# Attention with a routed expert layer on one core: fresh blocks for the last two sequences, expert groups begun at the end of attention, and the shared expert placed among later groups

## The chip, the cores and the metric

The kernel runs on one core of one Trainium2 chip. The metric is device time in microseconds of one launch. A core has five engines with queues of their own: TensorE (PE), VectorE (DVE), ScalarE (ACT), GpSimd (POOL) and SyncE (SP), which here only issues DMAs.

## The reference

A transformer block over x of 16 sequences x 256 tokens x 128 channels. First attention with 16 heads of 64 on the layer-normed input, then, on the layer norm of the sum, 160 routed experts, 8 per token, and one shared expert.

```python
x = x + attn(layernorm(x), Wq, Wk, Wv, Wo, bo)         # softmax over 256 keys per sequence
h = layernorm(x)
probs = sigmoid(h @ router_w.T + expert_bias)          # 4096 tokens x 160 experts
top_w, top_idx = top_k(probs, 8)
top_w = top_w / (sum(top_w) + 1e-9) * 2.5
routed = sum over the 8 chosen e of top_w[e] * (silu(h @ w_gate[e].T) @ w_down[e].T)   # inner size 64
shared = silu(h @ w_gate_shared.T) @ w_down_shared.T
x = x + routed + shared
```

## The kernel before

**Attention.** The first stage walks through 16 sequences b of 8 steps g, a step being two heads. All engines run a software pipeline written out by hand (`body(b)`): sequences 0 to 3 are unrolled, 4 to 15 are a loop, and three more calls, `body(B)` to `body(B + 2)`, drain it. With a lag of one sequence come the second layer norm (DVE, with rs by POOL), its transpose (L456), router logits (L462) and the choice of 8 experts (DVE `best`, `choose`); with a lag of two come the ranks (PE, `ranks`), the slot numbers (DVE `distances`, `new_blocks`, `slot_numbers`, `best_slots`), the state (`new_state`), the table of blocks (`blocks`), and the weights (`weights`).

**Slots.** Each token is copied to 8 slots of slot_x in DRAM, by POOL's indirect DMAs (`scatter`, L829, 16 per sequence). Slots are grouped in blocks of 64, a block belongs to one expert; a partly filled block is filled up by later sequences. There are 672 blocks (512 for full ones and 160 for leftovers). slot_x and block_y are cleared with zeros during attention, since unused slots are read too.

**Shared expert.** After attention, x transposed for the whole batch lies in SBUF (xn2T_res, written by ACT at L680). Eight chunks of 512 tokens go through two products, a Silu and an addition to x_res (L1161).

**Groups.** The blocks are computed in 84 groups of 8. For group n, SP loads 256 KB of slot_x (L341), PE transposes it (L594), ACT evacuates (L709), DVE copies the 8 experts' weights from w_all in SBUF into a ring of four (`weights_of`, L1183), PE multiplies (`gates`, L604), ACT applies Silu, PE multiplies again (`downs`, L615), ACT evacuates (L724), SP stores 256 KB to block_y (L346). PE's order for slot n is transposes(n), gates(n-1), downs(n-2). DVE may copy for group n when downs(n-4) is done. Four groups are a turn.

**Gathers and combines.** POOL gathers, for each of the 32 token tiles, 8 rows per token from block_y (`gather`, L852, 8 indirect DMAs) into yg, a ring of four tiles. Before sequence b's first tile it waits until groups up to 4b + 23 are stored. A gather into a ring place waits for the combine of the tile four before. DVE's combine(k) weighs and adds the 8 rows (L1190 to L1200); it stands in DVE's queue after turn COMBINE_FROM + k (COMBINE_FROM = 9), and those left over come after the last turn.

**What sets the order.** Each engine's order is its program's. w_all comes in 16 DMAs of 10 experts, the last five (E_EARLY = 50) after attention, because w_all lies where attention's buffers were. SP loads the first group only when all 16 sequences are scattered and routed (L329 to L333). DVE begins the copies after the shared expert, the table blk_i (L1171), and `output_rows`, which turns slot numbers into rows of block_y.

## Time and profile before

| | us |
|---|---|
| median of 3 runs | 1104.2 (1103.73 to 1104.58) |
| the profiled execution | 1104.33 |
| its span, first to last instruction | 1102.4 |
| PE busy | 831.2 (75%) |
| DVE busy | 758.8 (69%) |
| POOL busy | 704.4 (64%) |
| ACT busy | 673.1 (61%) |
| TensorE's mean granted clock | 0.877 |

The profile is of one execution. A timeline row gives start, length, engine, line, operation, result and operands, count, and in brackets the idle time of the engine before it and what ended it ("issue": nothing that the profile shows). Times count from the span's start. PEclk or "granted clock" is TensorE's clock as a share of full speed (1.00 is 2.4 GHz, 0.50 is 1.2 GHz).

### The profile page before, as it was taken

The numbers are of one execution on the slowest core, as the hardware profiler recorded it, in microseconds if no ns is written. First come the engines' busy times: TensorE is split into PE (matmuls) and PEld (weight loads), VectorE is DVE, ScalarE is ACT, GpSimd is POOL, SyncE is SP. The second block draws the span as 40 slices with busy tenths as digits, with TensorE's granted clock in tenths as the row PEclk, the third lists the DMA queues.
The fourth block names the chain that finished last, engine by engine and source line by source line (L and its number), as shares of the span: only waits on it lengthen the run. The fifth ranks groups of instructions, "written<-read, shape, count | busy, mean of one in ns | idle before, by whom it ended". The sixth has DMA issues, their size and how long they took to land.

```text
span 1102.4 us, 28627 instructions
## 1 busy us (share of the span) xinstructions
PE 831.2 (75%) x8062; PEld 640.1 (58%) x8062; DVE 758.8 (69%) x2574; ACT 673.1 (61%) x1997; POOL 704.4 (64%) x892
## 2 busy tenths in 40 slices
PE   4999999999999999999999968899776770000000
PEld 4777777777777777777777744677565560000000
DVE  4568878778887887887877875577887884223223
ACT  5888888888888888888888851377664550000000
POOL 2235677676776667767667667103777777777775
PEclk9999999999999999999999995699998885555555
DMA  8814422323333311221212123388887762112111
GB/s 261 328 40 157 154 106 100 144 109 133 143 143 120 118 64 62 75 84 65 93 64 68 55 110 151 129 268 278 284 254 228 227 223 76 57 57 57 57 57 50
DMA packets 62457, 144.61 MB, mean 131 GB/s; under 512 B 12496, under 2 KB 18576, under 8 KB 62416
## 3 DMA queue, kind: packets, MB, share of 16 engines
q1 hardware_dynamic: 46032, 110.56, 28.5%
q0 software_dynamic: 16384, 33.59, 10.0%
q8 instruction: 16, 0.26, 0.1%
q14 instruction: 25, 0.20, 0.1%
HBM read 59.16 MB, written 84.93 MB: 131 GB/s over the span
## 4 chain that ended last, share of the span: by engine, by line
PE 57%; POOL 17%; issue 11%; DMA 6%; DVE 6%; ACT 2%; DVEq 1%; SPq 0%; POOLq 0%; ACTq 0%
POOL yg L852 14%; PE psS L406 11%; PE psO L483 10%; PE psT L431 8%; PE psY L397 8%; PE psVM L397 5%; PE psA L443 4%; DMA block_y<-y_b 4%; PE psS L604 2%; POOL slot_x L829 2%; PE psT L553 1%; PE psT L594 1%; DMA xb<-slot_x 1%; DVE w_b L1183 1%; ACT y_b L724 1%
## 5 line engine op out<-in xcount | busy, mean ns | idle before, releaser
L852 POOL DMA_INDIRECT yg<-block_y,tok_idx x256 | 252.1, 985 | 137.6 <-issue 79.0
L829 POOL DMA_INDIRECT slot_x<-xn_src,slot_u x240 | 244.0, 1017 | 99.2 <-issue 52.7
L675 ACT ACTIVATE p_sb<-psS,negmax 128x256 f32<-128x256 f32 x512 | 236.0, 473 | 95.8 <-DVE negmax L1118 93.8
L789 POOL TENSOR_SCALAR p_sb<-p_sb,rinv 128x256 f32<-128x256 f32 x256 | 138.9, 550 | 128.4 <-DVE rinv L1073 125.9
L1118 DVE TENSOR_REDUCE negmax<-psS 128x2 f32<-128x512 f32 x256 | 164.2, 682 | 37.5 <-PE psS L406 37.3
L1183 DVE COPY w_b<-w_all 128x192 f32 x672 | 135.1, 272 | 34.7 <-issue 30.5
L406 PE MATMUL psS<-qk_sb 64*128 64x256 f32 x1024 | 145.2, 402 | 2.6 <-ACT p_sb L675 2.6
L483 PE MATMUL psO<-pT_sb,v_sb 128*64 128x256 f32 x1024 | 138.8, 391 | 7.5 <-issue 5.5
L279 ACT COPY pT_sb<-psT 128x512 f32<-128x512 f32 x256 | 140.5, 615 | 1.4 <-PE psT L431 1.4
L431 PE MATMUL psT<-ident,p_sb 128*128 128x128 f32 x1024 | 132.7, 272 | 0.0
L1190 DVE TENSOR_TENSOR yg<-yg,wE_res 128x1024 f32<-128x1024 f32 x32 | 39.1, 1222 | 126.5 <-DMA yg<-block_y,tok_idx 126.0
L431 PEld LDWEIGHTS psT<-ident,p_sb 128*128 128x128 f32 x1024 | 114.8, 140 | 1.2 <-issue 0.8
L483 PEld LDWEIGHTS psO<-pT_sb,v_sb 128*64 128x64 f32 x1024 | 65.1, 136 | 67.0 <-issue 36.8
L675 ACT ACTIVATION_READ_ACCUMULATOR p_sb<-psS,negmax 128x1 f32 x512 | 104.0, 203 | 0.0
L406 PEld LDWEIGHTS psS<-qk_sb 64*128 64x128 f32 x1024 | 88.5, 186 | 25.3 <-issue 7.8
L604 PE MATMUL psS<-xbT,w_b 128*64 128x64 f32 x1344 | 62.8, 241 | 34.1 <-issue 25.6
L651 ACT COPY qk_sb<-psY 128x512 f32<-128x512 f32 x128 | 76.1, 595 | 7.3 <-PE psY L397 4.9
L604 PEld LDWEIGHTS psS<-xbT,w_b 128*64 128x64 f32 x1344 | 51.2, 149 | 50.6 <-issue 44.5
L443 PE MATMUL psA<-wo_sb,oT_sb 128*128 128x128 f32 x512 | 79.5, 278 | 0.5 <-DVE oT_sb L1124 0.5
L667 ACT ACTIVATE p_sb<-p_sb,rinv 128x256 f32<-128x256 f32 x128 | 71.0, 555 | 0.0
L443 PEld LDWEIGHTS psA<-wo_sb,oT_sb 128*128 128x128 f32 x512 | 67.2, 191 | 2.0 <-DVE oT_sb L1124 1.0
L1073 DVE RECIPROCAL rinv<-rowsum 128x4 f32<-128x4 f32 x128 | 22.7, 177 | 66.3 <-ACT p_sb L675 62.8
(159 smaller groups left out, 1720.3 us busy)
## 6 DMA issues: line engine op xcount, KB each, us to landing
block_y<-zero SPq DMA_DIRECT2D x21, 1024.0 KB, 4.0
xb<-slot_x SPq DMA_DIRECT2D x84, 256.0 KB
block_y<-y_b SPq DMA_DIRECT2D x84, 256.0 KB
w_all<-in_wgd_dram SPq DMA_DIRECT2D x16, 960.0 KB
slot_x<-zero SPq DMA_DIRECT2D x1, 11264.0 KB, 40.9
slot_x<-zero SPq DMA_DIRECT2D x10, 1024.0 KB
yg<-block_y,tok_idx POOLq DMA_INDIRECT x256
slot_x<-xn_src,slot_u POOLq DMA_INDIRECT x240
```

The lines of the kernel that those rows point to most:

```text
L279: copy(pT_sb[:, (g - 3) % 2, h].rearrange("p a t -> p (a t)"), psT[:, h, :]).then_inc(s[f"pt{h}_ok"], 1)
L397: m = pe.matmul(dst, wsl[a], xsl[c], start=(n == 0), stop=(n == 2))
L406: m = pe.matmul(psS[:, h, qt * SEQ:(qt + 1) * SEQ], qk_sb[r, par, 0, qt * P:(qt + 1) * P], qk_sb[r, par, 1, :], start=True, stop=True)
L431: m = pe.transpose(psT[:, h, kt * SEQ + qt * P:kt * SEQ + (qt + 1) * P], p_sb[:, (g - 3) % 2, h, qt, kt * P:(kt + 1) * P], ident[:])
L443: m = pe.matmul(psA[:, 0, i * P:(i + 1) * P], oT_sb[:, (g - 4) % 2, i * P:(i + 1) * P], wo_sb[:, gp, :], start=(gp == 0 and i == 0), stop= ...
L483: m = pe.matmul(psO[h * DH:(h + 1) * DH, 0, 0:SEQ], v_sb[:, (g - 3) // 2 % 2, kt, (g - 3) % 2, h * DH:(h + 1) * DH], pT_sb[:, (g - 3) % 2, ...
L675: act.activation(p_sb[:, (g - 1) % 2, h, qt, :], psS[:, h, qt * SEQ:(qt + 1) * SEQ], ACT.Exp, bias=negmax[:, (g - 1) % 2, h, qt:qt + 1], s ...
L789: pool.tensor_scalar(pq, pq, rinv[:, (g - 2) % 2, k // 2, k % 2:k % 2 + 1], 1.0, ALU.mult, ALU.mult).then_inc(s["pn_ok"], 1)
L829: pool.indirect_dma_start(slot_x, bass.IndirectOffsetOnAxis(ap=slot_u[:, int(last), i, j:j + 1], axis=0), (xn2 if last else xn2_src)[:, i, ...
L852: pool.indirect_dma_start(yg[:, r, k, :], None, block_y, bass.IndirectOffsetOnAxis(ap=tok_idx[:, par, r, k:k + 1], axis=0)).then_inc(gat[r ...
L1118: dve.tensor_reduce(negmax[:, (g - 1) % 2, h, :], psS[:, h, :].rearrange("p (i k) -> p i k", i=TB), AX.X, ALU.max, negate=True).then_inc(s ...
L1183: m = dve.tensor_copy(w_b[:, r, i, :], w_all[:, bass.ds(e, 1), :].rearrange("p o i -> p (o i)"))
```

## The change

- The last two sequences (14, 15) get blocks of their own. `seal()` resets the state ahead of sequence 14's numbers: no block has room and numbering begins at FRESH = 160 + 14 x 32 = 608. There are 832 blocks, so 104 groups and 26 turns.
- SP loads the first groups when the scatters of sequences 0 to 13 have landed. Only at turn 9 it waits for the others (a semaphore of their own, scat_l). 20 experts instead of 50 are loaded late, and those in the last step of attention.
- The drain is cut to four steps of `body(B)`. What was left of it, transposes, logits, choice, ranks, slot numbers and weights of sequence 15, is written between groups 0 and 13. The table is made in two parts, columns for blocks 0 to 511 first, the rest at group 13; `output_rows` comes after group 10. The gathers of sequences 14 and 15 wait for all stores.
- x transposed is not kept in SBUF: ACT issues a DMA to DRAM (ffn_xT) instead of the copy at L680. The shared expert is done in 16 chunks of 256 tokens, one per turn from turn 9 on: SP loads a chunk, PE's two products are in r = 2 and r = 3, ACT's Silu in r = 2, DVE's addition in the next turn after the copy of r = 0, and PE's transposes of that r = 0 wait for the addition before.
- COMBINE_FROM is 10. The ring of w_b runs backwards in memory. Buffers are placed in another order, and three are aliased. Fills are denser. POOL computes rs of the second norm ahead of the scatter at g = 3.

```diff
-NBLK = T * TOPK // HB + E
+NBLK = T * TOPK // HB + 2 * E
-E_EARLY = 50
+E_LATE = 20
+SEALED = B - 2
+FRESH = E + SEALED * SEQ_BLK
-COMBINE_FROM = 9
+COMBINE_FROM = 10
+LEAD, LATE_RANKS, LATE_TABLE = 4, 5, 13
...
@@ sync @@
-                sp.wait_ge(s["s_ps"], 3 * i + 28)
+                sp.wait_ge(s["s_ps"], 2 * i + 28)
...
-                sp.wait_ge(s["s_ps"], 4 * i + 68)
+                sp.wait_ge(s["s_ps"], 3 * i + 60)
...
-            with sp.Fori(0, (E - E_EARLY) // 10) as i:
-                sp.wait_ge(s["s_ps"], 8 * i + 160)
+            with sp.Fori(0, (E - E_LATE) // 10) as i:
+                sp.wait_ge(s["s_ps"], 8 * i + 140)
...
+            sp.wait_ge(s["yq_ps"], NSTEP)
+            sp.wait_ge(s["v_ps"], G // 2 * B)
+            sp.wait_ge(s["xt_lo"], B + 1)
+            for i in range(E_LATE // 10):
+                sp.dma_start(w_all[:, 10 * i:10 * i + 10], wgd[:, 10 * i:10 * i + 10]).then_inc(s["we_in"], 16)
+            sp.wait_ge(s["scat"], 16 * SEALED * TB * TOPK)
-            sp.wait_ge(s["wr_ok"], B)
-            sp.wait_ge(s["be_ok"], B)
-            sp.wait_ge(s["st_ok"], 3 * B)
-            sp.wait_ge(s["x2r_ok"], B)
-            sp.wait_ge(s["scat"], 16 * NT * TOPK)
...
+            def turn(it, chunk=None):
                 for r in range(RING):
                     load_group(it, r, False)
                     store_y(RING * it + (r - STORE_LAG), (r - STORE_LAG) % 2)
+                    if r == 1 and chunk is not None:
+                        wait(sp, s["sh_ps"], chunk)
+                        sp.dma_start(xs, xT[bass.ds(chunk, 1)].rearrange("o p t -> (o p) t")).then_inc(s["xs_in"], 16)
@@ tensor @@
+            def shared_hidden(n):
+                pe.wait_ge(s["xs_in"], 16 * (n + 1))
+                pe.matmul(psT[0:INTER, 1, 0:SEQ], wgs_sb[:], xs, start=True, stop=True).then_inc(s["sh_ps"], 1)
+            def shared_out(n):
+                for i in range(TB):
+                    m = pe.matmul(psT[:, 0, i * P:(i + 1) * P], hs[:, i * P:(i + 1) * P], wds_sb[:], start=True, stop=True)
                 m.then_inc(s["sho_ps"], 1)
...
+            def experts(it, chunk=None):
                 for r in range(RING):
                     n = RING * it + r
+                    early = n if isinstance(n, int) else None
+                    if r == 0 and chunk is not None:
+                        wait(pe, s["shared_ok"], chunk)
+                    if r == RING - 1 and chunk is not None:
+                        pe.wait_ge(s["hs_ok"], chunk + 1)
+                    if early == LATE_RANKS + 1:
+                        pe.wait_ge(s["d_ok"], B)
+                    if early == LATE_TABLE + 1:
+                        pe.wait_ge(s["tab_ok"], 2)
                     transposes(it, r, n)
+                    if early == 0:
+                        continue
+                    if early == 1:
+                        ffn_transposes(B)
+                        logits(B)
+                        pe.wait_ge(s["p_ok"], 4 * NSTEP)
+                    gates((r - 1) % RING, n - 1)
+                    if early == LATE_RANKS:
+                        pe.wait_ge(s["mask_ok"], B)
+                        ranks(psT[:, (r - 1) % 2, :])
+                    if early == LATE_TABLE:
+                        pe.wait_ge(s["be_ok"], B)
+                        table(psT[:, (r - 1) % 2, :], TABLE_A, BC)
+                    if r == RING - 2 and chunk is not None:
+                        shared_hidden(chunk)
+                    if r == RING - 1 and chunk is not None:
+                        shared_out(chunk)
...
+                    downs((r - 2) % RING, n - 2)
@@ scalar @@
+            def keep_input(b):
+                wait(act, s["x2t_ok"], b)
+                act.dma_start(ffn_xT.rearrange("(b p) t -> b p t", p=D)[bass.ds(b - 1, 1)].rearrange("o p t -> (o p) t"),
+                              xn2T[:]).then_inc(s["x2_st"], 16)
@@ gpsimd @@
-                    if not is_last(b, 1) or g != 3:
-                        scatter(b, g)
                     if g == 3 and seq(b, 1):
                         inverse_deviation(b - 1, "ln2", mv2, ve2, rs2)
-                    if is_last(b, 1) and g == 3:
-                        scatter(b, g)
+                    scatter(b, g)
...
+                    late = isinstance(b, int) and b >= SEALED
                     for k in range(2):
-                        wait_apart(pool, sty[k], 8 * SEQ_BLK // GB * b + 8 * (E + SEQ_BLK) // GB)
+                        wait_apart(pool, sty[k], 8 * NGRP if late else 8 * SEQ_BLK // GB * b + 8 * (E + SEQ_BLK) // GB)
@@ vector @@
+            def seal():
+                dve.wait_ge(s["st_ok"], 3 * SEALED)
+                dve.tensor_scalar(room[:], ones_row[:], -HALF_UP, None, ALU.mult).then_inc(s["seal_ok"], 1)
+                dve.tensor_scalar(n_taken[:], ones_row[:, 0:1], float(FRESH), None, ALU.mult).then_inc(s["seal_ok"], 1)
...
+            def turn(it, chunk=None):
                 for r in range(RING):
                     weights_of(r, RING * it + r, False)
+                    if r == 0 and chunk is not None:
+                        shared(chunk)
...
+            weights(B)
+            ffn_norm(B)
+            dve.wait_ge(s["b_ps"], 1)
+            table(psY[:, 0, :], 0, TABLE_A)
+            dve.wait_ge(s["tab_ok"], 1)
+            dve.wait_ge(s["we_in"], 16 * (E // 10))
+            group(0)
+            biased(B)
+            group(1)
+            best(B)
+            blocks(B)
+            group(2)
+            choose(B)
+            group(3)
...
+            group(5)
+            distances(B + 1, psT[:, (LATE_RANKS - 1) % 2, :])
+            new_blocks(B + 1)
+            group(6)
+            slot_numbers(B + 1)
+            best_slots(B + 1)
+            group(7)
+            chosen(B + 1)
+            best_places(B + 1)
+            group(8)
+            blocks(B + 1)
+            group(9)
+            weights(B + 1)
+            group(10)
+            output_rows()
...
+            group(13)
+            dve.wait_ge(s["b_ps"], 2)
+            table(psT[:, (LATE_TABLE - 1) % 2, :], TABLE_A, BC)
```

## Rows read from the trace of the kernel before

**Rows 1.** Page, slices: POOL's busy tenths and the granted clock in 40 slices of 27.6 us.
```profile
POOL 2235677676776667767667667103777777777775
PEclk9999999999999999999999995699998885555555
```

**Rows 2.** Page, the chain that ended last, by line (share of the span).
```profile
POOL yg L852 14%; PE psS L406 11%; PE psO L483 10%; PE psT L431 8%; PE psY L397 8%; PE psVM L397 5%; PE psA L443 4%; DMA block_y<-y_b 4%; PE psS L604 2%; POOL slot_x L829 2%; PE psT L553 1%; PE psT L594 1%; DMA xb<-slot_x 1%; DVE w_b L1183 1%; ACT y_b L724 1%
```

**Rows 3.** Waits: who waited for whom, us in total, times, longest.
```profile
POOL yg L852 <- DMA block_y<-y_b: 58.1, 5, 54.8
PE psVM L456 <- DVE xn L894: 10.7, 13, 6.1
```

**Rows 4.** Timeline of POOL: last scatter; gathers of tiles 0, 4, 16, 20, and the last.
```profile
694.23 0.95 POOL L829 DMA_INDIRECT slot_x<-xn,slot_u  x1 [0.30 <-issue]
...
758.19 1.03 POOL L852 DMA_INDIRECT yg<-block_y,tok_idx  x1 [54.75 <-DMA block_y<-y_b]
...
799.70 1.03 POOL L852 DMA_INDIRECT yg<-block_y,tok_idx  x1 [0.27 <-POOL tok_idx L841]
...
931.17 1.89 POOL L852 DMA_INDIRECT yg<-block_y,tok_idx  x1 [1.64 <-issue]
...
973.33 0.97 POOL L852 DMA_INDIRECT yg<-block_y,tok_idx  x1 [1.35 <-issue]
...
1094.44 0.94 POOL L852 DMA_INDIRECT yg<-block_y,tok_idx  x1 [0.30 <-issue]
```

**Rows 5.** Timelines of POOL, DVE and PE around L456 in one sequence of attention.
```profile
580.10 1.05 POOL L829 DMA_INDIRECT slot_x<-xn_src,slot_u  x1 [0.17 <-DVE mv L887]
582.35 0.60 DVE L894 TENSOR_SCALAR xn<-x_res,mv,rs 128x128 f32 x2 [0.79 <-POOL rs L762]
583.01 0.44 PE L456 MATMUL psVM<-ident,xn 128*128 128x128 f32 x2 [0.29 <-DVE xn L894]
```

**Rows 6.** Timeline of DVE from the end of attention to the first groups.
```profile
654.34 0.25 DVE L887 BATCH_NORM_AGGREGATE mv<-st 128x2 f32<-128x6 f32 x2
658.71 0.60 DVE L894 TENSOR_SCALAR xn<-x_res,mv,rs 128x128 f32<-128x128 f32 x2 [4.13 <-POOL rs L762]
...
662.12 0.49 DVE L1102 TENSOR_TENSOR z_sb<-psVM,eb_sb 128x320 f32<-128x320 f32 x1
...
675.52 0.18 DVE L1058 TENSOR_TENSOR wE_res<-w_e,winv 128x16 f32<-128x16 f32 x1
...
701.06 0.29 DVE L1145 TENSOR_SCALAR yg<-pos_u 128x256 uint32<-128x256 uint32 x1
...
702.66 0.43 DVE L1156 TENSOR_TENSOR pos_u<-yg 128x256 uint32<-128x256 uint32 x1
```

**Rows 7.** Timeline of DVE, weight copies of groups 8, 23 and 28.
```profile
718.45 1.44 DVE L1183 COPY w_b<-w_all 128x192 f32 x8 [0.68 <-PE psA L615]
...
747.20 1.44 DVE L1183 COPY w_b<-w_all 128x192 f32 x8 [0.33 <-issue]
...
756.89 1.44 DVE L1183 COPY w_b<-w_all 128x192 f32 x8 [0.66 <-issue]
```

**Rows 8.** Timeline of DVE: a shared addition; the starts of combines 0, 3 and 11.
```profile
688.02 0.69 DVE L1161 TENSOR_TENSOR x_res<-psT,x_res 128x512 f32 x1 [3.21 <-PE psT L553]
...
780.91 1.22 DVE L1190 TENSOR_TENSOR yg<-yg,wE_res 128x1024 f32<-128x1024 f32 x1
...
812.74 1.21 DVE L1190 TENSOR_TENSOR yg<-yg,wE_res 128x1024 f32<-128x1024 f32 x1
...
906.60 1.23 DVE L1190 TENSOR_TENSOR yg<-yg,wE_res 128x1024 f32<-128x1024 f32 x1
```

**Rows 9.** Gates at either clock; window: PE, PEld, DVE, ACT, POOL busy, clock, DMA.
```profile
707.35 1.12 PE L604 MATMUL psS<-xbT,w_b 128*64 128x64 f32 x16
867.03 0.69 PE L604 MATMUL psS<-xbT,w_b 128*64 128x64 f32 x16 [3.00 <-issue]
781.00:910.00 129.00, 95.79 (x1657) 73.06 (x1652) 108.55 (x412) 71.46 (x187) 97.94 (x99) 0.88 0.75 238
```

More of the change, by code:

```diff
@@ L507, in values_read, with ffn_transposes, logits, ranks @@
                 wait(pe, s["v_ok"], min(G // 2 * b + n, G // 2 * B) if isinstance(b, int) else G // 2 * b + n)
[L509 removed]
+            def ffn_transposes(b):
+                wait(pe, s["ln2_xn"], TB * b)
                 for i in range(TB):
[L512 removed]
+                    m = pe.transpose(psVM[:, 0, i * P:(i + 1) * P], xn2[:, i, :], ident[:])
+                m.then_inc(s["x2t_ps"], 1)
+            def logits(b):
+                wait(pe, s["x2t_ok"], b)
+                for i in range(TB):
+                    m = pe.matmul(psVM[:, 0, i * E:(i + 1) * E], xn2T[:, i * P:(i + 1) * P], rw_sb[:],
+                                  start=True, stop=True)
+                m.then_inc(s["lg_ps"], 1)
+            def ranks(ps):
+                for i in range(TB):
+                    o = ps[:, i * E:(i + 1) * E]
                     m = pe.matmul(o, tri[:], mask[:, i, :], start=True, stop=(i == 0))
@@ L519, in ranks, with table @@
                 m.then_inc(s["rk_ps"], 1)
+            def table(ps, c0, c1):
+                for c in range(c0, c1):
+                    n = min(P, NBLK - c * P)
+                    m = pe.matmul(ps[:, (c - c0) * P:(c - c0) * P + n], blk_e[:, c:c + 1].broadcast_to([P, P]), ident[:, 0:n],
+                                  start=True, stop=True)
+                m.then_inc(s["b_ps"], 1)
             def input_transpose(b):
@@ new lines, in experts @@
+                    if early == 3:
+                        pe.wait_ge(s["ot_ok"], NSTEP)
+                        pe.wait_ge(s["x1_ok"], B)
+                    downs((r - 2) % RING, n - 2)
+            pe.wait_ge(s["pt0_ok"], NSTEP)
+            pe.wait_ge(s["pt1_ok"], NSTEP)
+            for it in range(LEAD):
+                experts(it)
+            with pe.Fori(LEAD, COMBINE_FROM - 1) as it:
+                experts(it)
+            experts(COMBINE_FROM - 1, 0)
+            with pe.Fori(COMBINE_FROM, TURNS - 1) as it:
+                experts(it, it - (COMBINE_FROM - 1))
@@ L921, in _, with biased @@
             dve.wait_ge(s["b_dve"], 1)
+            def biased(b):
+                wait(dve, s["lg_ps"], b)
+                wait(dve, s["den_ok"], b - 1)
+                dve.tensor_tensor(z_sb[:], psVM[:, 0, 0:TB * E].rearrange("p (i e) -> p i e", i=TB), eb_sb[:],
+                                  ALU.add).then_inc(s["z_ok"], 1)
             def best(b):
@@ L1018, in blocks @@
                 n = b - 1
-                first = bass.ds((b - 2) // 4, WIN)
+                late = isinstance(b, int) and b - 2 >= SEALED
+                first = bass.ds(WIN_LATE if late else (b - 2) // 4, WIN)
                 dve.tensor_copy(blk_w[:], blk_num[:, first]).then_inc(s["bw_ok"], 1)
@@ L1136, in body @@
                         choose(b)
-            sequences(dve, body)
+            for b in range(4):
+                body(b)
+            with dve.Fori(4, B) as b:
+                body(b)
+            body(B, 4)
             def output_rows():
```

310 lines of the change are left out of this document (145 added, 165 removed).

## Prediction

> **What bounds the kernel now.** I read the slices of the page first: PE at full clock up to slice 23, a gap of two slices at half clock, then the expert groups up to about 910 us, and from there only POOL busy (seven tenths and more) with PE idle [rows 1]. The chain of work that ended last says the same: POOL's gathers (L852) are its largest line [rows 2]. POOL waited once, 54.8 us, for the store of block_y, and then never for long again [rows 3]. The POOL timeline gives the skeleton [rows 4]: the last scatter begins at 694.23, the first gather at 758.19, the 256th and last at 1094.44. So the time is (start of the first gather) + (256 gathers) + (a rest of 1102.4 - 1095.4 = 7.0). 32 tiles of 8 gathers take 337 us: tiles 0 to 15, beside the groups, 931.17 - 758.19 = 173.0, or 10.8 each; tiles 16 to 31 take 164.2, or 10.26 each. Whatever moves the first gather moves the end, as long as nothing holds POOL later. Two things can: a gather of tile k+4 waits for combine k (four yg buffers), and the last tiles wait for the last groups' stores.
>
> The profiled execution took 1104.33 for a span of 1102.4, so 1.9 lie around it; the median is 1104.2. I sum in the span and add 1.9.
>
> **Part 1: attention.** PE is full there, so only a PE wait is worth anything. In each sequence DVE waits 0.79 us for POOL's rs before it writes xn2 (582.35), and PE then waits for xn2 (583.01); POOL starts a scatter at 580.10 ahead of ve and rs [rows 5]. The change puts inverse_deviation ahead of that scatter at g = 3. PE's wait at L456 is 10.7 us in 13 times, 6.1 of it the last [rows 3], so 4.6/12 = 0.38 per sequence. Moving rs by one scatter (1.3 us) covers it. I take 4 us off the end of attention (bounds: 0, if another wait takes its place, and 6). POOL's later scatters go 1.3 us later and have slack. ACT loses a copy per sequence (L680) and issues a DMA instead; ACT never issues a DMA in this trace, SP's issues take about as long as that copy did, so I take zero, bounds -0.4 to +0.4 per sequence on ACT, which has slack at g = 5. The zero fills grow (52 instead of 42 MB, and denser), but they go by DMA beside a PE that is full anyway: nothing. Aliases (moved, le, z_sb in place) only repeat orders that DVE's queue has already.
>
> **Part 2: the start of the groups.** Before, DVE copies the first weights after 703.09, the end of the slot arithmetic [rows 6]. In between lie the second layer norm (xn2 at 658.71), the last sequence's routing (662.12 to 675.7), and the shared expert. Now the groups start behind xn2. Work on DVE from there to the copy of group 23, in its written order:
> - xn2 done at 658.71 + 0.60 = 659.3, minus 4 of part 1: 655.3. The weights of the sequence before (1.3) fit into the 4.13 that DVE waits for POOL there [rows 6].
> - the first table, 0.7.
> - 24 groups: from 718.45 to 756.89 there are 20 in 38.4 us, 1.92 each [rows 7], so 46.1; the first one costs 1.5 more (registers, cold code).
> - routing of the last sequence: 13.6 less new_state (0.7), plus blocks(B) 1.6, output_rows 2.0, late table 0.3 [rows 6]: 16.8.
> - hand-overs where DVE has to wait until PE comes to ranks (group 5), the late table (group 13) and where PE waits in turn: bounds 0 and 10, taken as 4, two group times.
> Sum: 655.3 + 0.7 + 46.1 + 1.5 + 16.8 + 4 = 724.4. Before, group 23 was copied at 747.20 + 1.44 = 748.6 and the first gather came at 758.19, 9.5 later [rows 4, 7]; now PE is less behind, I take 8.6. **First gather at 733**, 25 us earlier; bounds 727 and 745. Table and weights are no limit: the last loads of w_all are issued in the last attention step. Nor is POOL: its scatter for the last sequence waits for slot numbers after group 6, about 680, and 16 scatters take 20 us.
>
> **Part 3: the coupled stretch.** DVE does four groups, then one combine. Combines start at 780.91 and, eleven rounds later, at 906.60: 11.43 us a round, and the last eight from 812.74 average 11.73 [rows 8]. POOL needs only 10.8 a tile, so DVE is slower than POOL, but before this lasted 12 rounds with a head start: combine 0 began 22.7 after the first gather, while tile 4 started 41.5 after it. The change takes from both sides. There are 20 more groups, so 16 rounds (26 turns less 10). COMBINE_FROM is 10: four more groups before combine 0, at (780.91 - 758.19)/11 = 2.07 each, 8.3, so combine 0 starts 31 + 0.3 after the first gather. And each round gains the shared chunk: half of an L1161 addition (0.69 for 512 columns [rows 8]), so 0.4, and 0.1 around it.
>
> A wait is new: at r = 0 PE's transposes wait for that addition, which stands on DVE behind the copy of group r = 0. Queued behind it on PE are gates and downs of the two groups before, which formerly ran under the combine; DVE's copies of r = 2 and 3 wait for those downs. Now PE stands idle 3.0 us for the first copy after the combine [rows 9]; it would be idle some 5 and start a slot later. With slots of 1.9 and copies of 2.0 the ring still just keeps up, so bounds of the cost per round are 0 and 2 and I take 0.1 to 0.2. **Round: 11.7 + 0.5 + 0.1 = 12.3.**
>
> Combine 15 is then through at 31.3 + 15 x 12.3 + 2.9 = 218.7 after the first gather. Unheld, POOL would start tile 19 at 173.0 + 3 x 10.5 + 1 = 205.5 [rows 4]. It is held back 13 us. From there 13 tiles at 10.26, 133.4, and the rest of 7.0.
>
> The last sequences' blocks cost nothing themselves: all 104 groups are stored some 230 after the first gather, tile 28 comes at 312. The fresh blocks mean only that many more groups. The removed shared stage (661 to 697) is in part 2 already.
>
> **Sum.** 733 + 218.7 + 133.4 + 7.0 = 1092.1 in the span, **1094.0** in time: 25 gained at the start, 15 given back in the rounds. The rounds decide: 15 x 1 us. Break-even is at a round of 12.3 + 10.3/15 = 13.0.
>
> **A rule weighed.** POOL's gathers beside copies: one row is 0.94 to 0.97 when alone, tiles beside the groups cost 0.5 more [rows 4]. The Trainium skill, "SBUF — State Buffer", section "SBUF: two separate sides", says that a DVE instruction such as an fp32 copy within SBUF locks GpSimd out of the port pair it needs for writing DMA descriptors, and the other way round, for the whole instruction. By that rule more groups beside gathers are a price of this change: tiles 16 to 19 at 10.8 instead of 10.26, 2 us. Since POOL is held anyway in those tiles, the sum stays; without holding it would be 2 us more, which the second rival contains.
>
> **Rivals.**
> (a) *PE's clock makes it the bound (slower).* Between 781 and 910 the granted clock was 0.88 on average, after PE had been busy 96 of 129 us; in the slices ahead of them, with steady groups, it was nine tenths or more [rows 1, 9]. At the lower of the two levels (1.2 GHz) 16 matmuls of L604 take 1.12 instead of 0.69 [rows 9], 1.6 times, so a slot 3.1 instead of 1.92. With the new wait PE has four slots after the addition and idles longer in one piece, so the clock should fall in more rounds. Then copy r = 3 waits for PE and the next addition for shared_out: 4 x 3.1 + 1.5 + 0.7 = 14.6 a round. If two rounds in three go so, the mean is 13.8: 1094 + 15 x 1.5 = **1116**. It decides from 13.0 on, a third of the rounds. Against it: a slow PE is a busy PE, and in the trace the clock came back each time. The Trainium skill, "TensorE: Matmul & The Clock Gate", section "HAM oscillation — how this bites in real kernels", describes this: bursts with waits between them are throttled anew in every iteration. Chance 0.17.
> (b) *Gathers alone are the bound.* If rounds stay under 11.7 (POOL held means fewer stretched copies), nothing holds POOL: 733 + 173.0 + 164.2 + 2 + 7.0 + 1.9 = **1081**. For it: copies take 1.44 per 8 before the gathers begin [rows 7]. Chance 0.17.
> (c) *The early start is eaten.* Hand-overs, cold straight-line code and half clock put the first gather at 745, the upper bound: **1106**. The 3.5 us that POOL once lost at new code, in the 4.13 of [rows 6], show such a price. Chance 0.14.
> (d) *The change doesn't hold the groups' early start at all* (DVE waits for the last w_all load): the sum is (c) or worse; 0.02, with (c).
> Forecast as it stands: 0.5, its own range 1086 to 1102.
>
> **How the numbers follow.** Range 1081 to 1108: from (b) to the beginning of (a). 0.2% (2.2 us, about what a measurement of this kernel can tell from no change) puts "same" at 1102.0 to 1106.4. Faster: forecast 0.49 + (b) 0.17 + a little of (a) and (c) 0.03 = 0.69. Same: 0.11, most of (c). Slower: 0.20, (a) and the end of (c).
>
> **What the profile will show.** First gather at 727 to 739 (part 2). PE without idle at L456 and attention's end 4 us earlier (part 1). Combines 31 us after the first gather and then every 12.3 (part 3), with POOL waiting for them from tile 8 or so, 13 us in all; the granted clock there 0.8 to 0.9. Wrong would be: a first gather after 745, rounds over 13 with a clock of 0.7, or POOL idle at its last tiles for stores.

## The result and the profile after

| | before | changed |
|---|---|---|
| median | 1104.04 (1103.73 to 1104.58) | 1122.48 (1118.91 to 1123.47) |
| ratio, 95% interval | | 1.0161 [1.0138, 1.0183] |
| span of the profiled execution | 1102.4 | 1120.5 |
| PE / DVE / POOL busy | 831.2 / 758.8 / 704.4 | 868.7 / 794.1 / 704.9 |
| granted clock | 0.877 | 0.893 |

The change makes the kernel slower by 1.6%. The forecast was 1094.0, and the time lies above the range's end of 1108. POOL's timeline shows the skeleton that the sum was built on, as in [rows 4]: first gather, tile 20, last gather.

```profile
720.40 1.01 POOL L909 DMA_INDIRECT yg<-block_y,tok_idx  x1 [25.71 <-DMA block_y<-y_b]
...
991.01 0.97 POOL L909 DMA_INDIRECT yg<-block_y,tok_idx  x1 [1.34 <-issue]
...
1112.53 0.95 POOL L909 DMA_INDIRECT yg<-block_y,tok_idx  x1 [0.30 <-issue]
```

The first gather is 37.8 us earlier than before, more than forecast. Tiles 4, 8, 12, 16 and 19 begin at 761.92, 814.06, 874.71, 936.19 and 977.53. Tiles 4 to 19 take 215.6 us for 15 tiles, 14.4 each, where before a tile took 10.8. So all that was gained at the start, and more, is lost again there. The page's slices, as in [rows 1], show both: the two slices at five and six tenths of the clock are now one at six tenths, and POOL is at five tenths in the middle of the gathers.

```profile
POOL 2236676767767676776767755277555454577775
PEclk9999999999999999999999968998887887855555
```

The chain that ended last, by line, as in [rows 2]:

```profile
PE psS L419 12%; PE psO L494 11%; PE psT L444 9%; PE psY L410 9%; POOL yg L909 9%; DVE w_b L1253 6%; PE psVM L410 5%; PE psA L456 5%; DVEq L249 3%; PE psS L603 3%; PE psT L593 3%; PE psY L614 2%; DVE yg L1260 2%; DVEq L1253 1%; DVE yg L1262 1%
```

POOL's gathers fell from 14% to 9% of it, and DVE's weight copies rose from 1% to 6%: through the coupled stretch the path now runs over DVE and the groups. The waits (who waits for whom: us in total, times, longest), as in [rows 3]:

```profile
POOL yg L909 <- issue: 93.7, 238, 9.7
PE psT L593 <- DVE x_res L1242: 69.2, 16, 9.1
DVE w_b L1253 <- issue: 49.4, 74, 5.6
POOL yg L909 <- DMA block_y<-y_b: 43.7, 7, 25.7
```

The second is the change's new wait: PE's transposes (L593) stand for 69.2 us in 16 times, 4.3 each, until DVE's addition (L1242) is done. Combines start at 755.53, 769.36, 782.86, 796.36, 810.11, 824.13, 837.86, 851.86, then 870.75, 885.42, 899.02, 913.09, then 932.23, 946.67, 960.30, 974.03. Two rounds, into combines 8 and 12, take 18.89 and 19.14 us; the other thirteen take 13.5 to 14.7, 13.88 on average. Forecast was 12.3 for all.

DVE's and PE's timelines over one ordinary round (the last instruction of a combine begins at 758.28; L1253 are the weight copies r = 0 to 3, L603 gates, L593 transposes, L578 shared_out, the second of the shared expert's two products):

```profile
756.04 0.71 PE L578 MATMUL psT<-wds_sb,x_res 64*128 64x128 f32 x4
759.03 1.67 DVE L1253 COPY w_b<-w_all 128x192 f32 x8 [0.45 <-issue]
760.62 0.41 DVE L1242 TENSOR_TENSOR x_res<-psT,x_res 128x256 f32<-128x256 f32 x1
761.26 1.11 PE L593 MATMUL psT<-ident,xb 128*128 128x128 f32 x4 [3.92 <-DVE x_res L1242]
761.33 1.45 DVE L1253 COPY w_b<-w_all 128x192 f32 x8 [0.29 <-issue]
762.30 1.12 PE L603 MATMUL psS<-xbT,w_b 128*64 128x64 f32 x16
764.41 1.11 PE L593 MATMUL psT<-ident,xb 128*128 128x128 f32 x4
765.29 1.66 DVE L1253 COPY w_b<-w_all 128x192 f32 x8 [2.51 <-PE psVM L614]
765.46 0.69 PE L603 MATMUL psS<-xbT,w_b 128*64 128x64 f32 x16
```

PE has nothing to do once the downs behind shared_out are through, although the gates of one group and the downs of the one before it are ready to run: they stand behind the transposes. After the addition PE runs its first slot at half clock (L603 takes 1.12, not 0.69; in all 15 rounds the first gates behind this wait take 1.09 to 1.12), a slot lasts 3.1 us, and DVE's copy r = 2 waits 2.51 us for the downs (L614) in it. This wait of DVE comes to 34.0 us in 17 times, the longest 2.6.

### The profile page after: what moved, and what is told of

It is laid out like the page before. It is cut to its first block, busy times and chain, and to the rows that moved or that the text cites. A ratio compares the mean times of both kernels' runs of the same rounds, so it can differ in the third digit from the quotient of the medians.

```text
span 1120.5 us, 30801 instructions
## 1 busy us (share of the span) xinstructions
PE 868.7 (78%) x8800; PEld 673.4 (60%) x8800; DVE 794.1 (71%) x2741; ACT 703.0 (63%) x2069; POOL 704.9 (63%) x892
## 4 chain that ended last, share of the span: by engine, by line
PE 61%; DVE 12%; POOL 10%; issue 10%; DVEq 5%; ACT 1%; DMA 0%; POOLq 0%; ACTq 0%
PE psS L419 12%; PE psO L494 11%; PE psT L444 9%; PE psY L410 9%; POOL yg L909 9%; DVE w_b L1253 6%; PE psVM L410 5%; PE psA L456 5%; DVEq L249 3%; PE psS L603 3%; PE psT L593 3%; PE psY L614 2%; DVE yg L1260 2%; DVEq L1253 1%; DVE yg L1262 1%
## 5 line engine op out<-in xcount | busy, mean ns | idle before, releaser
L1253 DVE COPY w_b<-w_all 128x192 f32 x832 | 171.0, 277 | 88.8 <-issue 49.4
L1195 DVE TENSOR_REDUCE negmax<-psS 128x2 f32<-128x512 f32 x256 | 164.3, 683 | 28.6 <-PE psS L419 28.4
L593 PE MATMUL psT<-ident,xb 128*128 128x128 f32 x416 | 80.2, 324 | 71.2 <-DVE x_res L1242 69.2
L751 ACT COPY xbT<-psT 128x512 f32<-128x512 f32 x104 | 61.5, 592 | 81.5 <-PE psT L593 81.2
L593 PEld LDWEIGHTS psT<-ident,xb 128*128 128x128 f32 x416 | 51.5, 160 | 93.5 <-issue 83.3
L603 PE MATMUL psS<-xbT,w_b 128*64 128x64 f32 x1664 | 82.5, 250 | 15.5 <-issue 8.1
L603 PEld LDWEIGHTS psS<-xbT,w_b 128*64 128x64 f32 x1664 | 67.8, 158 | 38.7 <-issue 32.8
L456 PE MATMUL psA<-wo_sb,oT_sb 128*128 128x128 f32 x512 | 78.8, 276 | 0.5 <-DVE oT_sb L1201 0.5
```

What stands on the lines that cost most here:

```text
L593: m = pe.transpose(psT[:, par, i * P:(i + 1) * P], xb[:, r, i, :], ident[:])
L603: m = pe.matmul(psS[half, par, cols], w_b[:, RING - 1 - r, i, 0:INTER], xbT[:, par, :, i * P // GB:(i + 1) * P // GB], start=True, stop=True)
L1195: dve.tensor_reduce(negmax[:, (g - 1) % 2, h, :], psS[:, h, :].rearrange("p (i k) -> p i k", i=TB), AX.X, ALU.max, negate=True).then_inc(s ...
L1253: m = dve.tensor_copy(w_b[:, RING - 1 - r, i, :], w_all[:, bass.ds(e, 1), :].rearrange("p o i -> p (o i)"))
```

## Experiments

Ratios are to the kernel before on the same chip, which took 1103.7 (numbers 1, 3, 4, 5), 1104.1 (2, 6, 7, 8) and 1103.6 (9, 10). "Ordinary" rounds are those other than into combines 8 and 12. The changed kernel itself was measured once, beside the kernel before at 1104.04; where an experiment is compared with it, the two come from different chips. PE has a last wait for the additions ahead of the last turn; it is written apart and stays in experiments 4, 8, 9 and 10, so the round into combine 15 still has it there (13.70, 14.13, 14.66 and 14.41 us).

**1. POOL's order in attention alone.** In the kernel before:

```diff
-                    if not is_last(b, 1) or g != 3:
-                        scatter(b, g)
                     if g == 3 and seq(b, 1):
                         inverse_deviation(b - 1, "ln2", mv2, ve2, rs2)
-                    if is_last(b, 1) and g == 3:
-                        scatter(b, g)
+                    scatter(b, g)
```

> The kernel before with one edit: POOL computes rs of the second norm ahead of the scatter at g = 3. In the changed kernel a sequence of attention takes 39.0 us instead of 39.65, 10 us in all. Theory A: the order on POOL brings all of it: 39.0 per sequence and about 1094.5 in time, since the later stages only shift. Theory B: ACT's copy that became a DMA brings the part over my 0.38 per sequence: 39.3 here and about 1098.5.

1098.15, ratio 0.9939 [0.9916, 0.9962]. A sequence takes 39.30 instead of 39.65, the last layer norm's aggregate comes at 648.62 instead of 654.34 [rows 6], the first gather at 752.80. So this edit gives the 0.35 a sequence that the forecast had worked out (0.38), and no more: the changed kernel's 39.0 has a second cause.

**2. ACT's copy replaced as well.** Experiment 1, and in it the copy of L680 becomes a DMA that ACT issues (whoever waits for it counts to 16 a sequence, and ACT waits for it before it writes xn2T again):

```diff
-                        act.copy(xn2T_res[:, bass.ds((b - 1) * SEQ, SEQ)], xn2T[:]).then_inc(s["x2r_ok"], 1)
+                        act.dma_start(xn2T_res[:, bass.ds((b - 1) * SEQ, SEQ)], xn2T[:]).then_inc(s["x2r_ok"], 16)
```

> As the run of this kernel before, at the usual speed: the kernel before with rs first and ACT's copy as a DMA. Theory A (the copy is the rest of attention's gain): 39.0 per sequence, 1093.5. Theory B: 39.3, 1098.

1090.33, ratio 0.9884 [0.9856, 0.9912]; a sequence takes 39.05, the aggregate comes at 646.53, the first gather at 746.91. ACT's copy is the second cause, 0.25 a sequence. What it cost were PE's small gaps: between 194 and 620 us PE is busy 421.00 of 426 us in experiment 1 and 424.07 here (the columns are PE, PEld, DVE, ACT, POOL busy, clock, DMA share, GB/s).

```profile
194.00:620.00 426.00, 421.00 (x3347) 330.94 (x3346) 348.41 (x1152) 363.51 (x1118) 300.96 (x412) 1.00 0.28 99
```

```profile
194.00:620.00 426.00, 424.07 (x3372) 333.87 (x3370) 351.09 (x1165) 362.93 (x1118) 303.66 (x415) 1.00 0.29 103
```

Of the 5.9 us by which the first gather comes earlier than in experiment 1, 2.1 lie ahead of the aggregate. The other 3.8 fall between it and the gather; their cause is not shown.

**3. No chunks among the groups.** In the changed kernel the 16 chunks, their waits and loads are taken out of the turns, so the shared expert is missing from the output:

```diff
-                    if r == 0 and chunk is not None:
-                        wait(pe, s["shared_ok"], chunk)
...
-                        shared_hidden(chunk)
...
-                        shared_out(chunk)
...
-                    if r == 0 and chunk is not None:
-                        shared(chunk)
```

> The changed kernel without the shared expert among the groups (its sum is left out: no chunk loads, no products, no Silu, no additions, no wait of PE). Theory A (PE's wait for the addition makes the rounds long): rounds fall from 13.9 to 11.5 to 11.8 and the time by 15 x 2 = 30 us or more, to 1085 or less. Theory B (16 rounds beside 20 more groups are slow by themselves, by clock or DMA): rounds stay at 13 or more, time over 1105. Theory C, on the two rounds of 19: if the longer loop body of DVE makes them, they go with the additions (the body is then as in the kernel before), another 10 us less; if they come from the loop's start over alone, they stay.

1082.36, ratio 0.9806 [0.9787, 0.9825]. Ordinary rounds take 11.48, the two long ones 14.72. The rounds are long because of the chunks; the two longer ones exist without them, though shorter than with them (18.89 and 19.14).

**4. No wait of PE.** DVE's addition reads x_res alone, so the shared sum is missing from the output; the products, the Silu and an instruction of DVE in the addition's place stay:

```diff
-                    if r == 0 and chunk is not None:
-                        wait(pe, s["shared_ok"], chunk)
...
-                dve.tensor_tensor(xr, psT[:, 0, 0:SEQ].rearrange("p (i d) -> p i d", i=TB), xr, ALU.add).then_inc(s["shared_ok"], 1)
+                dve.tensor_tensor(xr, xr, xr, ALU.max).then_inc(s["shared_ok"], 1)
```

> The changed kernel, all of its shared work kept, but DVE's addition reads x_res alone instead of PSUM (the shared sum is left out of the output), so PE's transposes need not wait for it. Theory A (the wait is the cost): rounds 12.0 to 12.4 apart from the two long ones, time about 1122 - 13 x 1.6 = 1101, and the granted clock between the combines higher. Theory B (the additions, products and the Silu themselves are the cost, or the clock falls anyway under the combines): rounds over 13, time over 1113. The two rounds of 19 stay in any case.

1090.97, ratio 0.988 [0.9851, 0.9909]. Ordinary rounds 11.83, long ones 16.44 and 16.58; combine 0 to combine 15 takes 186.9 us instead of 218.5. Of the 39.8 that experiment 3 takes off this stretch, 31.6 are the wait, and 8.2 the chunks' own work, 0.55 a round. The time is lower than either theory had it, and so are the rounds. The window from combine 0 to combine 15 speaks on the clock; the changed kernel first, then this one:

```profile
755.53:974.03 218.50, 150.14 (x2258) 111.48 (x2260) 147.36 (x571) 99.53 (x256) 121.94 (x128) 0.83 0.63 194
```

```profile
756.36:943.23 186.87, 143.98 (x2258) 106.30 (x2259) 147.61 (x572) 98.09 (x255) 125.06 (x129) 0.86 0.74 228
```

The mean clock rises from 0.83 to 0.86. The mean alone does not tell how long a round is: over the same stretch it is 0.85 in experiment 3, with ordinary rounds of 11.48, and 0.94 in experiment 9, with 12.95.

**5. The addition ahead of the copy.** DVE's order alone, nothing left out:

```diff
                 for r in range(RING):
-                    weights_of(r, RING * it + r, False)
                     if r == 0 and chunk is not None:
                         shared(chunk)
+                    weights_of(r, RING * it + r, False)
```

> The changed kernel with DVE's addition ahead of the copy for r = 0 instead of behind it, nothing left out. Theory A: PE's wait ends a copy and its register loads earlier, 2 to 3 us; the round falls from 13.9 to 12.4 to 12.9 and the time by 15 to 22 us, to 1100 to 1108. Theory B (the wait is not what counts): no change, 1120 or more; or worse, if DVE then waits for shared_out.

1088.46, ratio 0.9871 [0.984, 0.9902]. Ordinary rounds 11.63, long ones 15.25 and 15.45. One instruction moved ahead of a copy of 1.7 us takes 34 us off the changed kernel and makes it faster than before, by more than the 15 to 22 us that theory A had. PE still waits for the addition, 42.4 us in all instead of 69.2, but DVE's waits for downs (L614, whichever PSUM tile they write) come to 4.5 us instead of 38.1, and the clock between combines 0 and 15 is 0.90.

**6. DVE's loop written out.** In the changed kernel:

```diff
-            with dve.Fori(1, (TURNS - COMBINE_FROM) // YR) as q:
+            for q in range(1, (TURNS - COMBINE_FROM) // YR):
```

> As the run of this kernel before, on a chip where the kernel before should take its usual 1104: DVE's loop over the coupled rounds written out. Theory A (the loop's start over costs 5.3 and 5.6): both long rounds fall to 13.9, time 1112. Theory B: they stay, 1122. In the run where everything was slow the rounds at combines 8 and 12 were no longer than the others, 19.4 and 19.6, which speaks for A.

1109.54, ratio 1.0055 [1.0036, 1.0074]. The rounds into combines 8 and 12 take 13.85 and 14.04, like the others (13.62). DVE's timeline shows what is gone. The first copies after combines 7 and 11 in the changed kernel:

```profile
860.28 1.67 DVE L1253 COPY w_b<-w_all 128x192 f32 x8 [5.26 <-issue]
...
921.89 1.55 DVE L1253 COPY w_b<-w_all 128x192 f32 x8 [5.64 <-issue]
```

and those after combines 7 and 11 with the loop written out:

```profile
859.77 1.69 DVE L1253 COPY w_b<-w_all 128x192 f32 x8 [0.46 <-issue]
...
913.98 1.57 DVE L1253 COPY w_b<-w_all 128x192 f32 x8 [0.58 <-issue]
```

**7. Both, 5 and 6.**

> As the run of this kernel before, at the usual speed: addition ahead of the copy of r = 0 and DVE's loop written out. Theory A: 6 to 7 less than with the addition ahead alone (1088.5), so 1082. Theory B, straight-line code costs as much as the loop's start over: 1088.

**1072.85, ratio 0.9713 [0.9682, 0.9745]**: 2.9% faster than before and 4.4% faster than the changed kernel. All 15 rounds average 11.16. The two edits give 51.2 us of the 218.5 between combines 0 and 15; singly they gave 36.6 and 13.5. The time is some 9 us below the 1082 of theory A. The start of tile 20:

```profile
942.03 0.97 POOL L909 DMA_INDIRECT yg<-block_y,tok_idx  x1 [1.34 <-issue]
```

Tile 20 begins 220.3 after the first gather (721.73), where the changed kernel's begins 270.6 after; from the start of the first gather to that of the last it is 341.0 us, where before it was 336.3 [rows 4]. POOL is hardly held. This is the second rival's case (gathers alone are the bound), reached with another order.

**8. PE's wait half filled.** 16 transposes of the identity, into a part of psT that nobody reads then, ahead of the wait in each turn of the loop:

```diff
+                    if r == 0 and chunk is not None and not isinstance(it, int):
+                        pe.wait_ge(s["xt2_ok"], n)
+                        for _ in range(16):
+                            pe.transpose(psT[:, 1, 0:P], ident[:], ident[:])
                     if r == 0 and chunk is not None:
                         wait(pe, s["shared_ok"], chunk)
```

> As the run of this kernel before, at the usual speed: 16 transposes ahead of PE's wait. Theory A (clock): L603 behind the wait takes 0.69 instead of 1.1, rounds fall by 1.0 to 1.5 and the time to 1100 to 1108. Theory B (latency of the handover): rounds stay at 13.9 or grow, 1122 or more.

1118.18, ratio 1.0123 [1.009, 1.0155]; ordinary rounds 13.55, clock 0.89 over the stretch. In the ordinary rounds 1.6 to 3.3 us of the wait were left, and in about half of them the clock still fell, at once or one slot later. Neither theory's number, so this run decides nothing.

**9. PE's wait filled.** The same with `range(32)`.

> The kernel of g1_busy_32 again, on another chip, for the same reason: 32 transposes of the identity ahead of PE's new wait in each coupled turn, which fill it; order unchanged. Theory Q: ordinary rounds 13.4 to 14.0 and 1114 to 1126, although the gates behind the wait take 0.69 us. Theory C: ordinary rounds 12.8 or less, 1106 or less.

1111.09, ratio 1.0059 [1.0042, 1.0077]. PE's and DVE's timelines over one round (L626 are the transposes put in; lines of DVE carry L1257 and L1246 here):

```profile
785.80 3.71 PE L626 MATMUL psT<-ident 128*128 128x128 f32 x32
787.45 1.91 DVE L1257 COPY w_b<-w_all 128x192 f32 x8 [0.47 <-issue]
789.28 0.41 DVE L1246 TENSOR_TENSOR x_res<-psT,x_res 128x256 f32<-128x256 f32 x1
789.92 0.65 PE L593 MATMUL psT<-ident,xb 128*128 128x128 f32 x4 [0.40 <-DVE x_res L1246]
790.50 0.69 PE L603 MATMUL psS<-xbT,w_b 128*64 128x64 f32 x16
792.59 1.76 DVE L1257 COPY w_b<-w_all 128x192 f32 x8 [1.46 <-PE psVM L614]
```

In the ordinary rounds, the last one apart, PE waits 1.8 us at most, the first gates behind the wait take 0.69 in all but one, and the clock over the stretch is 0.94. DVE's copy r = 2 still waits for the downs, 1.46 us here instead of 2.51. Ordinary rounds take 12.95, or 12.8 without the last, whose wait is not filled. That is between the theories: the order alone forecast 13.4 to 14.0, the clock alone 12.8 or less, and the time, too, is between 1106 and 1114. Holding the clock is worth 0.93 a round, or 1.1 without the last.

**10. The wait moved behind gates and downs.** PE's order in r = 0 of a turn with a chunk, DVE's as in the changed kernel:

```diff
                     if r == 0 and chunk is not None:
+                        gates((r - 1) % RING, n - 1)
+                        downs((r - 2) % RING, n - 2)
                         wait(pe, s["shared_ok"], chunk)
+                        transposes(it, r, n)
+                        continue
```

> The kernel of g2_wait_later again, on another chip: there the kernel before itself took 1258.68 and every kernel's rounds were near 20 us, so that nothing about the wait could be read. The edit: PE's new wait kept, but in the turns with a chunk the gates of r = 3 and the downs of r = 2 of the turn before are issued ahead of it, the transposes of r = 0 behind it; nothing left out. Theory Q (order: the downs behind the wait are what costs): ordinary rounds 11.9 to 12.5, time 1088 to 1098. Theory C (clock after the idle time): ordinary rounds 13.2 or more, time 1110 or more.

1097.98, ratio 0.9956 [0.994, 0.9973]; ordinary rounds 12.27, as the theory of the order forecast. One round:

```profile
783.79 1.67 DVE L1257 COPY w_b<-w_all 128x192 f32 x8 [0.45 <-issue]
785.38 0.41 DVE L1246 TENSOR_TENSOR x_res<-psT,x_res 128x256 f32<-128x256 f32 x1
785.73 3.48 DVE L1257 COPY w_b<-w_all 128x192 f32 x16
786.03 1.06 PE L593 MATMUL psT<-ident,xb 128*128 128x128 f32 x8 [2.87 <-DVE x_res L1246]
```

PE still waits, 2.87 us. The clock between combines 0 and 15 is 0.87, a little over the changed kernel's 0.83 and well under experiment 9's 0.94. But the copies r = 1 and r = 2 now run in one piece behind the addition: what copy r = 2 needs was done under the combine.

**11. The same edits where the kernel before is slow.** In two further sets of runs the kernel before itself took 1256.5 us (the first four below) and 1258.7 us (the last three). The record numbers their chips 10 and 2, and it gives the number 2 to experiments 9 and 10 as well, where the kernel before took 1103.6 some minutes later. So it is not shown that the chip makes the difference, although the expectations of 9 and 10 speak of another chip. The edits are those above: the loop written out (6), with the addition first (7), the wait half filled (8), ACT's DMA (2), the wait filled (9), the wait moved (10), and 7 and 10 together.

> The changed kernel with DVE's loop over the coupled rounds 4 to 15 written out, nothing left out. DVE stood 5.3 and 5.6 us idle where that loop starts over (combines 8 and 12), and 3.3 longer than usual still without the additions. Theory A (going back to the loop's start costs it, as code is fetched anew): both go, combine to combine 13.9 throughout, time 10 us less, 1112. Theory B (something else comes in every fourth round, such as the slot copy of POOL or a DMA): they stay, 1122.

1.0245 [1.0203, 1.0287].

> The changed kernel with DVE's addition ahead of the copy of r = 0 and DVE's loop written out. In the run with the addition ahead alone the long rounds were 15.3 and 15.5 against 12.0. If both effects are separate: 3.3 x 2 = 6.6 less than that run, 1082 in time; if the fetch of straight-line code costs as much as the loop's start over, 1088 as there.

1.022 [1.0178, 1.0262].

> The changed kernel with 16 transposes of the identity into a PSUM bank that is free at that time, which PE does just ahead of its wait for DVE's addition, in the coupled turns: PE is then idle for a shorter piece. Theory A (the long wait costs through the clock: at 1.2 GHz the first slots behind it take 2.7 instead of 1.9, and DVE's copy of r = 2 waits 2.2 for them): the clock stays up, L603 behind the wait takes 0.69, rounds fall by 1.0 to 1.5, time 1100 to 1108. Theory B (the handover's latency costs it at any clock): rounds stay at 13.9, or grow by what the transposes delay, time 1122 or more.

1.0335 [1.0291, 1.0378].

> The kernel before with rs first (as in the first run) and ACT's copy of xn2T in each sequence replaced by a DMA that ACT issues, within SBUF. Theory A (the rest of attention's gain, 0.3 per sequence, is ACT's copy): 39.0 per sequence instead of 39.3, end of attention 4.5 us earlier, time 1093.5. Theory B (something else of the change brings it): 39.3, 1098.

0.9966 [0.9948, 0.9984].

> The changed kernel with 32 transposes of the identity (they write to a part of psT that nobody reads then) ahead of PE's new wait in each coupled turn, twice as many as in f3_busy_wait; 16 of them took 1.97 us there at half clock, and 2.09 us of waiting were left, so 32 fill the wait of 3.7 to 3.9 us nearly. Theory Q (queue: the wait costs because the gates and downs of the two groups before stand behind it, and DVE's copy r = 2 needs those downs; the clock hardly matters): ordinary rounds stay at 13.4 to 14.0 and the time at 1114 to 1126. Theory C (clock: the wait costs because PE stands idle in one piece and then runs its first slots at the lower level): slots behind the wait have gates of 0.69 us, ordinary rounds come down to 12.8 or less, the time to 1106 or less.

1.0401 [1.0379, 1.0423]. (The expectation calls 1.97 us for 16 transposes half clock; four of L593 take 0.65 in the same rounds and 1.11 at the lower level, so 1.97 is full clock.)

> The changed kernel with PE's new wait kept, but in the turns with a chunk the gates of r = 3 and the downs of r = 2 of the turn before are issued ahead of it, and the transposes of r = 0 behind it; DVE's order is that of the changed kernel, nothing is left out. Theory Q: the downs that copy r = 2 needs are done under the combine, its wait (2 to 2.5 us) is gone; ordinary rounds 11.9 to 12.5 as without the wait (11.9), time 1088 to 1098. Theory C: PE still stands idle for about 2.5 us or more in one piece and restarts at the lower level; ordinary rounds stay at 13.2 or more, time 1110 or more.

1.026 [1.0223, 1.0297].

> f2_both (addition ahead of copy r = 0, DVE's loop written out) and PE's wait moved behind gates and downs as in g2_wait_later; nothing left out. In f2_both POOL was nearly never held, so both theories expect about the same time: 1066 to 1073, rounds 10.8 to 11.2. Over 1076 would mean that the transposes of r = 0 have become late for ACT and for the gates one slot on.

1.0279 [1.0235, 1.0324].

The rounds of the last three and of the first take 17 to 22 us. PE's gates are broken up there by idle time in which it waits for nothing that the profile shows. With the loop written out, gates come in pieces:

```profile
966.07 0.85 PE L603 MATMUL psS<-xbT,w_b 128*64 128x64 f32 x16
968.96 0.80 PE L603 MATMUL psS<-xbT,w_b 128*64 128x64 f32 x9
970.48 0.34 PE L603 MATMUL psS<-xbT,w_b 128*64 128x64 f32 x4 [0.72 <-issue]
971.90 0.34 PE L603 MATMUL psS<-xbT,w_b 128*64 128x64 f32 x3 [1.07 <-issue]
```

What makes these gaps was not tried, so these ratios say little about the causes above. They do say that the gain of experiment 7 does not hold everywhere: under these conditions its kernel is 2.2% slower than before.

## Why the prediction was wrong

In the sum's own terms, of the profiled execution:

| term | forecast | measured | difference |
|---|---|---|---|
| first gather | 733 | 720.4 | -12.6 |
| from there to combine 0 | 31.3 | 35.1 | +3.8 |
| 15 rounds | 184.5 | 218.5 | +34.0 |
| combine 15 to tile 19 | 2.9 | 3.5 | +0.6 |
| 13 tiles | 133.4 | 136.0 | +2.6 |
| rest | 7.0 | 7.0 | 0 |
| span | 1092.1 | 1120.5 | +28.4 |

The skeleton held: POOL is held by combine 15, and from there on the tiles run alone. Two steps failed, both in the 15 rounds: 13 x (13.88 - 12.3) = 20.5 for the new wait, 2 x (19.0 - 12.3) = 13.4 in the two long rounds, of which some 3 are the same wait and 10 something that the sum did not contain. That the first gather came 12.6 early was not forecast either; without it the miss would have been larger by as much.

**The price of PE's wait (part 3).** The forecast named the right thing, gates and downs of two groups behind the wait and copies r = 2 and 3 behind those downs, had bounds of 0 and 2 for it, and took 0.1 to 0.2. Measured by experiment 4, it is 31.6 us in 15 rounds, 2.1 each, just over the upper bound. (The round without it was forecast at 11.7 + 0.5 = 12.2 and ordinarily took 11.83; that hid a part of the error.) The step that failed is "with slots of 1.9 and copies of 2.0 the ring still just keeps up". The ring has no slack there: what ran under the combine (3.0 us) and copy r = 0 (1.7) are two slots that the wait moves out of it, and they then come one after the other with copies that need them. Two runs split the 31.6. With the wait left and the order changed (10), 27.4 are gone; with the order left and the clock held (9), 13.2 are gone. Together that is 9 more than the whole, since they overlap: a slot at half clock costs DVE something only while DVE waits for it. So the order carries 18.4 to 27.4 of the 31.6, and the lower clock after the wait 4.2 to 13.2, the upper end being the 0.9 a round of experiment 9. That a slot at half clock counts only there is argued from the rows, not tried by itself.

**The start over of DVE's loop (nowhere in the sum).** DVE stands idle for 5.26 and 5.64 us where its loop over q starts over. Written out (6), both are gone. The kernel before had such a loop too. It started over once, after combine 7, and there DVE's gap was small, so no row of before showed this price (its other first copies after a combine wait 0.5 to 1.3):

```profile
865.21 1.73 DVE L1183 COPY w_b<-w_all 128x192 f32 x8 [1.56 <-issue]
```

In the changed kernel without chunks (3), whose loop holds the same kinds of instructions as the one before, the gaps are 4.32 and 4.27. So the additions in the body are at most a part of it; why the loop before was cheap stays open. The Trainium skill, "Runtime: NRT & Kernel Launch", section "Instruction fetch mechanics", says that instructions are fetched ahead in sequence and that a taken branch whose target is not in the current window makes the engine wait for a fetch. By that rule a body of four turns and four combines pays at each start over, if it is longer than the window, and straight code does not; the changed kernel agrees, the loop of before shows that it need not be so.

**The rivals.** (a) gave 1116 from a mean round of 13.8 and is closest in number, but its mechanism holds by half only: PE is busy 150.14 of the 218.5 us between combines 0 and 15 and is not the bound, DVE's wait is for downs behind the wait (r = 2, not r = 3 as the rival had it), and the clock there was 0.83, where the forecast had named 0.7 as the sign of this rival. Experiment 9 gives its share, 0.93 a round of the 1.58 that the ordinary rounds were over the forecast, and part of that share goes with the order as well. The rule of the Trainium skill cited there ("TensorE: Matmul & The Clock Gate", section "HAM oscillation — how this bites in real kernels"), that bursts with waits between them are throttled anew in each iteration, agrees with the round above (1.12 behind a wait of 3.92) and with what filling the wait takes away (0.69). (b) was right on what lies below: with both edits the time is 1072.85, where its 1081, less the 11.3 by which that run's first gather (721.73) came before 733, is 1069.7. (c) went the other way, and (d) did not come about: the first copy of weights begins at 648.36.

**Part 2, the first gather.** It came 12.6 before the forecast, outside its bounds (727 to 745). The last layer norm's aggregate came at 644.03, 10.3 earlier than before and not 4:

```profile
646.00 0.60 DVE L951 TENSOR_SCALAR xn<-x_res,mv,rs 128x128 f32<-128x128 f32 x2 [0.50 <-POOL rs L818]
...
648.36 1.65 DVE L1253 COPY w_b<-w_all 128x192 f32 x8 [1.16 <-issue]
...
710.78 1.44 DVE L1253 COPY w_b<-w_all 128x192 f32 x8 [0.54 <-issue]
```

That is 6.3 more than the forecast had. From the aggregate to the end of xn2 it is 2.57 us instead of 4.97, since DVE waits 0.50 for POOL where it had waited 4.13 [rows 6]: 2.4 more. From the end of xn2 (646.6) to the end of group 23's copy (712.2) there are 65.6 us instead of 69.1, and the gather follows 8.2 later instead of 8.6: -3.9. 6.3 + 2.4 + 3.9 = 12.6.

**Part 1, attention.** The size of POOL's order was right (experiment 1: 0.35 a sequence, forecast 0.38). The step that failed is ACT's: for a DMA issue in place of a copy the forecast took zero between bounds of -0.4 and +0.4, and experiment 2 gives 0.25 to the good. "PE is full there, so only a PE wait is worth anything" was too strict: no wait of PE for ACT stood among the long ones, yet PE's idle time between 194 and 620 us fell by 3.1 us with that copy gone.

**Part 3, the rest.** The chunk's own work was right: 0.55 a round (forecast 0.5). Combine 0 came 3.8 later after the first gather, since from group 23's copy to it there are 20 groups in 44.75 us, 2.24 each, instead of 2.07. The 13 tiles took 2.6 more: tile 19 itself takes 13.5.

**The rule weighed.** The prediction weighed the Trainium skill's rule on the port that DVE and GpSimd share ("SBUF — State Buffer", section "SBUF: two separate sides"). Copies take 1.44 before the first gather (710.78) and mostly 1.6 to 1.7 beside gathers, so they are longer by a sixth, which agrees in kind. Of the gathers no run shows a price: the changed kernel's tiles 0 to 2, beside copies, take 10.09, 10.05 and 10.12 us, and most tiles take 10.0 to 10.3 alone. With both edits tiles 12 to 14, where POOL is not held, take 10.47, 10.26 and 10.52, so the 2 us that the prediction set for four tiles is an upper bound. It decided nothing.

## What to carry to other kernels

Ask of a new wait not only how long it is but what stands behind it in its engine's queue, and who needs that; then put in front of it whatever does not need it (10), or let the instruction that it waits for run first (5). When the path runs through an engine's loop of long straight bodies, look for a gap at its start over, and write the loop out where it shows. A price between bounds of 0 and 2 us that is paid in every round is the forecast itself: here the range had to reach to 15 x 2 on the slow side.

## What the runs showed of the hardware

- A start over of DVE's loop took 5.26 and 5.64 us, and 4.32 and 4.27 in the kernel without chunks; the kernel before had 1.56 at the start over of a loop of the same kind.
- After 3.92 us without work TensorE ran its next slot at the lower of its two levels (16 gates in 1.12 us instead of 0.69), although over the whole stretch it had work for 69% of the time. With 3.71 us of transposes in such a wait it ran at full clock behind it (0.69).
- A DMA issued by ACT in place of a copy within SBUF made a sequence of attention 0.25 us shorter, on a PE without a long wait.
- The same kernel before took 1256.5 and 1258.7 us in two sets of runs and 1103.6 to 1104.1 in the others, and one chip number stands in the record for both (1258.7, then 1103.6). In the slow sets gates of the changed kernel's variants came in pieces, with idle time in which the engine waited for nothing that the profile shows.
- Weight copies of DVE took 1.44 us before POOL's gathers began and mostly 1.6 to 1.7 beside them.
